# A Mamba, FP4 and attention layer in one kernel: three elementwise steps go to GpSimd, bias rows in one pass, fewer waits, and a new order on every queue

## The reference

```
xn = layernorm(x)
s  = mamba_block(xn)          # u = ln(xn)*g1+b1; xi, z = split(u @ in_proj); xc = silu(conv4(xi) + b)
                              # dt = softplus(...); h[t] = exp(dt*A)*h[t-1] + (dt*xc)[t]*B[t], 16 states
                              # y = sum_n h*C + D*xc; xn + (y*silu(z)) @ out_proj, then LN and a gelu FFN
g  = fp4_ffn(xn)              # inputs and hidden values quantized in blocks of 16; silu(gate)*up; down
x  = x + s * silu(g)
xn = layernorm(x)
s  = attention(xn)            # 16 heads; it attends over the batch axis, which has 2 entries
g  = three_residual_blocks(xn)# LoRA-folded linear + bias, LN, gelu, linear, bias, + residual
x  = x + s * silu(g)
```

## Time and profile before

| | |
|---|---|
| median of 3 runs | 1848.96 us (1847.87 to 1852.0) |
| profiled execution, its own time | 1856.52 us |
| its span, first to last instruction | 1854.7 us |
| PE busy | 1577.4 us, 85% |
| DVE busy | 1551.4 us, 84% |
| ACT busy | 1437.5 us, 78% |
| POOL busy | 1252.4 us, 68% |
| mean granted TensorE clock | 0.953 |
| rows of B and C: landing after issue | 3.3 us, 256 issues |

### The profile page before, as it was taken

How to read it: one execution, slowest core, us unless ns; L and a number is a source line. 1 busy time by engine, 2 the same in 40 slices (tenths; PEclk the granted TensorE clock), 3 DMA queues, 4 the chain that set the end, 5 groups by cost and what they waited for, 6 DMA issues and landing times.

```text
span 1854.7 us, 28175 instructions
## 1 busy us (share of the span) xinstructions
PE 1577.4 (85%) x7632; PEld 1164.4 (63%) x7632; DVE 1551.4 (84%) x2882; ACT 1437.5 (78%) x3076; POOL 1252.4 (68%) x1313
## 2 busy tenths in 40 slices
PE   0083768899999999999989999999989999999875
PEld 0051556586767677776767676767667767767653
DVE  0623999999999999999999999999999999999811
ACT  0034678898989898989889888989888989888723
POOL 0304676777777786868687777778686868787522
PEclk9976789999999999999999999999999999999987
DMA  8000111111111111111111111111111211111100
GB/s 209 0 6 29 52 47 58 47 57 37 58 48 60 43 52 51 59 47 52 52 52 52 44 51 50 58 47 46 58 52 47 63 41 58 46 44 55 35 0 12
DMA packets 68395, 91.70 MB, mean 49 GB/s; under 512 B 15674, under 2 KB 34686, under 8 KB 68238
## 3 DMA queue, kind: packets, MB, share of 16 engines
q1 hardware_dynamic: 68238, 89.91, 15.8%
...
## 4 chain that ended last, share of the span: by engine, by line
PE 27%; POOL 20%; DVE 16%; issue 16%; ACT 12%; POOLq 0%; ACTq 0%; DVEq 0%; DMA 0%
PE bank L511 10%; POOL drive L965 10%; PE bank L627 6%; DVE unit L1127 4%; DVE hc L1133 3%; PE bank L516 2%; PE y_ps L537 2%; ACT unit L742 2%; PE bank L498 1%; PE bank L563 1%; ACT op_a L709 1%; DVE xc L1158 1%; ACT L709 1%; ACT L923 1%; POOL s L1068 1%
## 5 line engine op out<-in xcount | busy, mean ns | idle before, releaser
L965 POOL TENSOR_TENSOR drive<-wx,rows 128x1024 f32<-128x1024 f32 x256 | 604.1, 2360 | 163.3 <-DVE unit L1127 82.8
L1127 DVE TENSOR_TENSOR_SCAN unit<-unit,drive 128x512 f32<-128x512 f32 x512 | 616.7, 1221 | 30.7 <-POOL drive L971 23.4
L742 ACT ACTIVATE unit<-dt,aneg 128x254 f32<-128x254 f32 x1024 | 441.9, 468 | 19.8 <-ACT carry L750 0.7
L1133 DVE TENSOR_TENSOR hc<-unit,rows 128x512 f32<-128x512 f32 x512 | 340.9, 684 | 8.8 <-issue 3.0
L537 PE MATMUL y_ps<-ident,hc 128*128 128x128 f32 x2048 | 278.1, 282 | 52.5 <-DVE hc L1133 52.4
L537 PEld LDWEIGHTS y_ps<-ident,hc 128*128 128x128 f32 x2048 | 241.2, 145 | 115.3 <-DVE hc L1133 71.8
L742 ACT ACT_TABLE_LOAD x109 | 139.8, 1283 | 3.7
L750 ACT ACTIVATE carry<-unit 128x4 f32<-128x4 f32 x512 | 79.3, 169 | 66.8 <-DVE unit L1140 63.0
L627 PE MATMUL bank<-op_a,w_f 128*128 128x256 f32 x512 | 115.7, 385 | 11.2 <-ACT op_a L709 11.2
L709 ACT ACT_TABLE_LOAD x77 | 98.8, 1283 | 22.4 <-PE bank L498 21.6
L511 PE MATMUL bank<-w_f,wide 128*128 128x256 f32 x512 | 113.3, 379 | 1.5 <-ACT wide L709 1.5
...
## 6 DMA issues: line engine op xcount, KB each, us to landing
rows<-rows_scratch SPq DMA_DIRECT2D x256, 256.0 KB, 3.3
...
```

What stands on the lines that cost most here:

```text
L742: last = a_.activation(u[:, k * TOK:(k + 1) * TOK].rearrange("p (b t) -> p b t", b=B)[:, :, 1:TC], dt[p][:, g, :].rearrange("p (b t) -> p ...
L965: g_.tensor_tensor(drive[n % 2][:, :, :].rearrange("p (g b) t -> p g b t", b=B), wx[p][:, :, :].rearrange("p g (b t) -> p g b t", b=B), ro ...
L1127: v.tensor_tensor_scan(u[:, :], u[:, :], d, 0.0, ALU.mult, ALU.add).then_inc(S["scan_done"], 1)
L1133: v.tensor_tensor(hc[n % NPROD][:, 4 * half:4 * half + 4, :].rearrange("p (g b) t -> p g b t", b=B), unit_of(ch, n, half)[:, :].rearrange( ...
```

## The change

- `wx` (dt*xc) is now a step of POOL. The addition of v to the context is the POOL step `cadd`, the addition to x the POOL step `xadd`; DVE's statistics of x become a step `x1s` that waits for it. A semaphore `ctx_ready` takes the place of the eighth count of `attn_dve`.
- A bias row is a matmul over 64 rows in the type F32R: rows 0 to 5 of `b_two` hold the biases, rows 32 to 37 what rounding them to that type leaves, and `pick` selects both. The preparation has four more loads, a memset and five small DVE instructions for it.
- Waits that an earlier instruction of the same queue implies are left out: `dt_ready` but for the first exp, `wx_ready` but for drive 0, `carry_in` but for states 0 and 8, `drive_ready` and `y_summed` in the b halves, `rows_in` at `hc`.
- All five plans are new. Everything of the arithmetic and of the buffers stays.

```diff
@@ -72,37 +73,38 @@
 
 
 PE_PLAN = """
-    b0a-- xp kv-- sum8- dt0 hqT0- q-- b0T-- sum9- v1-- dt1 b0b-- sum10- hqT1- hqT2- sum11- ctxT-- h1T-- b2b---
-    b1a-- sum12- sum13- dn- sum14- b1T-- sum15- ao-- xqT ygT0- skip ygT1- g00 sum0 g01 op- g10 sum1 g11 b1b--
-    u00 u01 sum2 u10 u2T- u11 sum3 h2T-- f10- f11- f12- f13- b2a-- uT+ sum4 sum5 f2- b2T-- xi0+ xi1+ sum6 z0+
-    sum7 xn1T- xi2+ xi3+ z1+
+    xi3 z1 b0a-- kv-- xp sum8- hqT0- dt0 q-- b0T-- sum9- v1-- hqT1- dt1 sum10- b0b-- sum11- h1T-- hqT2- ctxT--
+    b1a-- sum12- b2b--- sum13- dn- sum14- b1T-- sum15- ao-- ygT0- ygT1- skip xqT op- g00 g01 sum0 u00 b1b-- u01
+    sum1 g10 g11 u10 u2T- sum2 u11 sum3 h2T-- f10- f11- sum4 f12- f13- uT+ b2a-- sum5 f2- b2T-- xi0+ xi1+ sum6
+    sum7 z0+ xn1T- xi2+
 """
 ACT_PLAN = """
-    exp12a- hq1- hq2- out11a- exp12b- out11b- h1-- exp13a- ctx-- out12a- out12b- exp13b- out13a- exp14a- exp14b-
-    usave dtln gatec--- out13b- exp15a- out14a- exp15b- first out14b- exp0a b1n-- gatem- b1g-- out15a- exp0b
-    out15b- s1-- yg0- xq exp1a out0a out0b exp1b yg1- exp2a out1a exp2b g00 out1b g01 exp3a out2a exp3b g10
-    out2b g11 exp4a out3a opn- out3b exp4b xn+ xhf+ u2- h2-- exp5a out4a exp5b f10- f11- out4b f12- exp6a out5a
-    f13- exp6b out5b u+ exp7a b2n-- out6a exp7b out6b exp8a out7a exp8b b2g-- tap0+ tap1+ hn- z0+ xn1- tap2+
-    tap3+ z1+ out7b out8a xc0+ xc1+ exp9a exp9b out8b exp10a b0n- kv- xp+ out9a out9b exp10b exp11a dt0+ out10a
-    exp11b hq0 b0g- aexp- dt1+ out10b v1- dtexp+
+    out10b- dtexp hq1- h1-- exp12a- out11a- out11b- exp12b- exp13a- hq2- out12a- out12b- exp13b- ctx-- exp14a-
+    dtln out13a- b1n-- out13b- exp14b- exp15a- out14a- exp15b- gatec--- gatem- b1g-- first s1-- out14b- yg0-
+    out15a- yg1- exp0a exp0b out15b- xq exp1a out0a exp1b g00 out0b out1a g01 usave exp2a exp2b out1b exp3a opn-
+    g10 out2a g11 out2b exp3b exp4a u2- out3a out3b exp4b h2-- out4a xn+ exp5a exp5b f10- xhf+ f11- f12- out4b
+    f13- exp6a out5a exp6b out5b exp7a u+ out6a exp7b b2n-- out6b exp8a out7a exp8b b2g-- tap0+ tap1+ out7b hn-
+    z0+ tap2+ out8a xn1- tap3+ z1+ xc0+ xc1+ exp9a out8b exp9b exp10a kv- out9a exp10b out9b b0n- xp+ hq0 out10a
+    exp11a dt0+ exp11b b0g- aexp- v1- dt1+
 """
 POOL_PLAN = """
-    drive14- drive15- b1-- arg fix0 drive0 xout fin--- drive1 drive2 hb1-- drive3 fix1 f+ drive4 op- drive5 j0in
-    hb2-- drive6 s0b- drive7 b2-- drive8 j0out j1in x1- drive9 drive10 diff- j1out b0- hb0- drive11 xin+ drive12
-    drive13 log+
+    drive13- cadd-- log b1-- drive14- drive15- wx arg fin--- xout fix0 drive0 drive1 drive2 op- hb1-- drive3
+    drive4 f+ drive5 j0in s0b- drive6 fix1 j0out drive7 b2-- j1in drive8 xadd- hb2-- x1- drive9 hb0- diff-
+    drive10 j1out b0- drive11 xin+ drive12
 """
 DVE_PLAN = """
-    clr15a- xround yg- scan0a clr15b- hc0a scan0b clr0a hc0b clr0b scan1a hc1a clr1a scan1b scan2a hc1b clr1b
-    hc2a scan2b clr2a hc2b op- clr2b scan3a scan3b h2-- hc3a hc3b clr3a clr3b ug0 scan4a scale0 ug1 hc4a scan4b
-    clr4a hc4b scan5a clr4b scan5b hc5a xscale+ hc5b clr5a clr5b round0 scan6a b2s-- hc6a scale1 scan6b clr6a
-    hc6b scan7a hc7a clr6b scan7b clr7a hc7b clr7b x1- scan8a conv0+ scan8b hc8a hc8b clr8a conv1+ round1 b0s-
-    clr8b scan9a scan9b hc9a hc9b clr9a clr9b scan10a hc10a scan10b clr10a scan11a score- scan11b hc10b hc11a
-    clr10b hc11b clr11a attn- clr11b h1- scan12a hc12a scan12b hc12b clr12a clr12b scan13a hc13a clr13a f++
-    scan13b b1s- hc13b clr13b scan14a scan14b hc14a hc14b clr14a clr14b dt+ scan15a wx+ scan15b hc15a hc15b
+    scan12b- hc12b- scan13a- b1s-- hc13a- clr12a- clr12b- scan13b- f+ clr13a- hc13b- clr13b- dt scan14a-
+    scan14b- hc14a- hc14b- clr14a- scan15a- clr14b- scan15b- hc15a- hc15b- clr15a- yg- xround clr15b- scan0a
+    scan0b hc0a clr0a hc0b op- scan1a hc1a scan1b clr0b hc1b clr1a h2-- clr1b scan2a scan2b ug0 hc2a scan3a hc2b
+    clr2a clr2b scale0 hc3a clr3a scan3b hc3b clr3b scan4a ug1 hc4a scan4b clr4a hc4b scan5a hc5a clr4b scan5b
+    hc5b clr5a xscale+ round0 scan6a hc6a b2s-- clr5b clr6a scale1 scan6b hc6b clr6b scan7a hc7a scan7b clr7a
+    x1- hc7b x1s- scan8a clr7b scan8b hc8a conv0+ hc8b clr8a conv1+ round1 clr8b b0s- scan9a scan9b hc9a clr9a
+    hc9b clr9b scan10a scan10b hc10a clr10a scan11a score- scan11b hc10b hc11a hc11b clr10b clr11a attn- h1-
+    scan12a clr11b hc12a
 """
 SP_PLAN = """
-    rows8- rows11- load+ rows10- rows12- rows13- wr rows14- rows15- rows0 rows1 rows3 rows2 store--- rows4
-    again- rows6 rows5 rows9 rows7
+    rows5-- rows7-- rows6-- rows8-- rows10-- rows9-- again--- rows12-- rows11-- load rows13-- wr- rows15--
+    rows0- rows14-- rows3- rows2- store---- rows1- rows4-
...
-    x_diff=1, attn_dve=8, attn_exp=2, final_ready=2, stored=16,
+    x_diff=1, attn_dve=7, ctx_ready=1, attn_exp=2, final_ready=2, stored=16,
...
-        b_rows = sb("b_rows", [NROW, D])
+        b_rows = sb("b_rows", [2 * LOW, D])
+        b_two = sb("b_two", [2 * LOW, D], F32R)
+        pick = sb("pick", [2 * LOW, LOW], F32R)
...
+                *[piece for r in (0, LOW) for piece in (
+                    (b_rows[r:r + 3, :], biases.rearrange("(i k) d -> i k d", k=2)[:, 0, :]),
+                    (b_rows[r + 3:r + 4, :].rearrange("o (h d) -> o h d", d=HD),
+                     qkv_b.rearrange("(h c d) -> c h d", c=3, d=HD)[0:1, :, :]),
+                    (b_rows[r + 4:r + 5, :].rearrange("o (h d) -> o h d", d=HD),
+                     qkv_b.rearrange("(h c d) -> c h d", c=3, d=HD)[2:3, :, :]),
+                    (b_rows[r + 5:r + 6, :], ao_b[None, :]))],
...
+                    nc.gpsimd.memset(b_two[:, :].bitcast(F32), 0.0).then_inc(c_done, 1)
...
+                    v.tensor_copy(pick[0:LOW, :], ident[0:LOW, 0:LOW]).then_inc(c_prep, 1)
+                    v.tensor_copy(pick[LOW:2 * LOW, :], ident[LOW:2 * LOW, LOW:2 * LOW]).then_inc(c_prep, 1)
+                    dve.wait_ge(c_done, 6)
+                    for r in (0, LOW):
+                        v.tensor_copy(b_two[r:r + NROW, :], b_rows[r:r + NROW, :]).then_inc(c_prep, 1)
+                    dve.wait_ge(c_prep, 6 * len(quants) + 7)
+                    v.tensor_tensor(b_two[LOW:LOW + NROW, :], b_rows[LOW:LOW + NROW, :],
+                                    b_two[LOW:LOW + NROW, :].bitcast(F32), ALU.subtract).then_inc(c_prep, 1)
...
             def bias_row(dst, row, wide_):
-                return t.matmul(dst[:, 0:wide_ * D], ident[0:NROW, row:row + 1].to_broadcast([NROW, P]),
-                                b_rows[:, None, :].to_broadcast([NROW, wide_, D]), start=False, stop=True,
+                return t.matmul(dst[:, 0:wide_ * D], pick[:, row:row + 1].to_broadcast([2 * LOW, P]),
+                                b_two[:, None, :].to_broadcast([2 * LOW, wide_, D]), start=False, stop=True,
                                 skip_group_check=True)
...
             elif name == "ctxT":
-                pe.wait_ge(*at("attn_dve", ch))
+                pe.wait_ge(*at("ctx_ready", ch))
                 turn(dst, token_blocks(ctx_), "ctxT_full")
...
             if name[:3] == "exp":
                 n, half = int(name[3:-1]), "ab".index(name[-1])
                 u = unit_of(ch, n, half)
-                act.wait_ge(*at("dt_ready", ch))
+                if (n, half) == (0, 0):
+                    act.wait_ge(*at("dt_ready", ch))
                 act.wait_ge(*at("carry_saved", ch, 2 * n + half + 1 - NUNIT))
...
             elif name[:3] == "out":
                 n, half = int(name[3:-1]), "ab".index(name[-1])
                 act.wait_ge(*at("unit_clear", ch, 2 * n + half + 1))
-                act.wait_ge(*at("carry_in", ch, 1 + n // 8))
+                if n % 8 == 0 and half == 0:
+                    act.wait_ge(*at("carry_in", ch, 1 + n // 8))
...
             elif name == "v1":
                 act.wait_ge(*full("v1", ch))
-                act.wait_ge(*at("attn_dve", ch - 1))
+                act.wait_ge(*at("ctx_ready", ch - 1))
                 a_.activation(v1[:, :], dense("v1", ch)[:, 0:D], ACT.Copy).then_inc(S["v1_copied"], 1)
...
             if name[:5] == "drive":
                 n = int(name[5:])
                 pool.wait_ge(*rows_in(ch, n))
-                pool.wait_ge(*at("wx_ready", ch))
+                if n == 0:
+                    pool.wait_ge(*at("wx_ready", ch))
                 pool.wait_ge(*at("scan_done", ch, 2 * n - 2))
...
                 pool.wait_ge(*at("drive_ready", ch, 2 * n + 1))
-                pool.wait_ge(*at("carry_in", ch, 1 + n // 8))
+                if n % 8 == 0:
+                    pool.wait_ge(*at("carry_in", ch, 1 + n // 8))
                 g_.tensor_tensor(drive[n % 2][:, :, 0], drive[n % 2][:, :, 0], fix[:, n, :], ALU.add)\
                     .then_inc(S["drive_ready"], 1)
+            elif name == "wx":
+                pool.wait_ge(*at("dt_ready", ch))
+                pool.wait_ge(*at("xc_ready", ch))
```

(41 more changed lines are left out.)

6 lines of the change are left out of this document (removed).

## The result

The changed kernel takes 2121.1 us (four runs, 2119.95 to 2133.73) against 1849.5 us before: ratio 1.148, 95% interval 1.144 to 1.153. The forecast was 2065, with its own range 2025 to 2110 and the stated one 1985 to 2130.

What follows compares the result with a forecast made beforehand. DVE's queue was taken as the kernel's clock: 96.15 - 2.6 + 19.85 = 113.4 us a repeat, 13.75 more. Fifteen repeats (206) and the last chunk (+10) gave 2072.5, stated as 2065, own range 2025 to 2110, stated range 1985 to 2130.

Steps and rivals of the forecast that it cites:

- A: At scan0a, after xround: DVE has only a clear while POOL runs xout, fix0, drive0 and its carry addition; 3.95 us.
- B: At scan2a: ACT needs 2.98 us after clr1a, DVE has h2 and a clear, 0.75; a stall of 2.25 us.
- D: At scan5a: ACT's out, xn and exp after clr4a take 2.12 us against one DVE product, 0.69; 1.45 us.
- F: At x1s, DVE's statistics of x: waits for POOL's addition and two hand-overs, behind hc7b; 0.8 us.
- G: At conv1: PE's xi2 and taps and ACT's xn1 copy after conv0, about 2.7 us against DVE's 1.06; 1.65 us.
- I: At scan12a, directly after h1: PE's transposes, ACT's copy and exp, and a bank that ACT frees late; 2.65 us.
- L: At scan14b: ACT's 7.35 us after exp13b, including a load between Ln and exp, against DVE's about 5.4; 1.95 us.
- M: At yg, straight after hc15b: DVE waits for PE's last sum, where xround stood between before; 1.05 us.
- small: Three smaller stalls of DVE, at scan3b, scan6a and attn, estimated together at 1.35 us a repeat.
- Rival 2: PE's granted clock falls to about 0.79, stalls holding matmuls grow: a repeat of 118 us or more, 2135; chance 0.12.
- Rival 1: Same direction, smaller: only the forced stalls, some shortened by leaner waits; a repeat of 109.5 us, 2007; chance 0.18.
- the others: Faster, DVE's shorter list decides: 1807 us, chance 0.06; or no change, most stalls covered by each other: 1849, chance 0.03.

Runs made afterwards that it cites:

- Experiment 1: The changed kernel's work in the five plans of the kernel before, with only the three moved steps placed: 1878.0 us, ratio 1.0135 to the kernel before.
- Experiment 5: Changed kernel with SyncE issuing the second load of x first in its period instead of behind five row loads: 2137.4 us, ratio 1.155.
- 8: The changed kernel's work in the order of the kernel before, with dt*xc kept on DVE and both additions on POOL: 1856.3 us, ratio 1.0009.
- 4: Changed kernel with one step moved on POOL, xout behind drive0 instead of ahead of fix0: 2156.7 us, ratio 1.165.
- 6: Changed kernel with ACT's two exponentials of state 12 ahead of the last down-projection copy and the copy of h1: 2126.4 us, ratio 1.149.
- 7: Changed kernel with DVE's rounding of x (xround) ahead of the gating of y (yg): 2134.4 us, ratio 1.152.
- 10: Changed kernel with conv0 on DVE ahead of clr7b, scan8b and hc8a: 2124.7 us, ratio 1.148.
- 11: Changed kernel with the second load of x first, state 12's exponentials and conv0 earlier, and 44 zero matmuls on PE: 2110.3 us, ratio 1.140.

## Why the prediction was right, and where it was off

The mechanism was right: the new orders leave DVE without work between a clear and the scan that needs ACT's or POOL's answer to it. Experiment 1 shows it from outside, the stalls from inside. The time itself came in with some luck: 2121 lies above the forecast's own range (2025 to 2110) and 9 us inside the stated one, and one of the four runs, 2133.73, lies outside it. The predicted slowdown, 216 us, is four fifths of the measured 272. Per step, in the short repeat:

```
step            A    B    D    F    G    H    I    J    K    L    M    small
predicted, us  3.95 2.25 1.45 0.8  1.65 1.1  2.65 0.5  1.15 1.95 1.05 1.35
measured, us   3.98 2.30 1.38 2.04 3.76 1.07 2.46 0.30 1.14 1.57 1.12 1.05
```

(L is 0.71 before dt and 0.86 before scan14b; small is what is left of 22.2.)

*The size.* Predicted 19.85 us of stalls and a repeat of 113.4, measured 22.2 and 115.9, and 117.1 as the mean of the 13. Two terms were mis-sized. **F** was 0.8 and is 2.04: I costed SyncE's order at 0, but `again`, the second load of x, stood behind six row loads that wait for hc, was issued at 1386.49, and POOL's addition to x waited for it until 1390.66. Experiment 5 took away just that 1.2 us. **G** was 1.65 and is 3.76: the transposes and xi2, xi3 behind conv0 ran at a granted clock of 0.50, after PE had idled 3.62 us, and xi2 and xi3 took 3.70 us instead of 1.94. The remaining 1.2 us to the mean are mostly repeats in which the clock fell at other places as well.

The rows for F, of SyncE and POOL:

```profile
1386.49 0.39 SPq L1297 DMA_DIRECT2D x<-in_L_attn_x_dram  x1
```

```profile
1390.66 1.28 POOL L1079 TENSOR_TENSOR x<-x,s 128x512 f32<-128x512 f32 x1 [2.35 <-DMA x<-in_L_attn_x_dram]
```

And for G, PE in the short repeat, its window, and the same step in the long repeat:

```profile
1397.86 1.12 PE L512 MATMUL bank<-ident,h 128*128 128x128 f32 x4 [3.62 <-DVE xc L1194]
1398.77 3.70 PE L577 MATMUL bank<-u_t,w_in 128*128 128x262 f32 x8
```

```profile
1397.00:1400.00 3.00, 2.14 (x7) 1.93 (x8) 1.85 (x6) 0.76 (x2) 1.09 (x2) 0.50 0.03 11
```

```profile
1163.48 1.94 PE L577 MATMUL bank<-u_t,w_in 128*128 128x262 f32 x8
```

The changed kernel holds its own test of this. In its three long repeats, where xi2 and xi3 ran at full clock and took 1.94 us, DVE waits 1.71 us before the conv, which is the 1.65 of the prediction; in the other ten it is 3.2 to 3.8. So the chain of G was priced rightly, and its error is the clock.

*Off DVE.* I gave the three moved pieces their full 2.6 us. Experiments 1 and 8 show that in the order before they return nothing, and in the changed kernel it is about half: there the addition that makes dt takes 2259 ns beside a drive, 1225 before, and DVE's busy time fell by 20 us, not 42. This error is in the term "- 2.6" of the repeat; in the repeat of the table dt happened to take 1.22 (there it was POOL's drive that took 3.43 instead of 2.36), which is why the sum still fits. In 12 of the 16 chunks dt takes 2.4 us or more.

*Bias rows.* I took a quarter of the time; it is half: 96 rows take 47.4 us, where 192 records took 100.9. For the end of the run that made no difference, because in the changed kernel PE has 21 us idle a repeat. In the order before, it is worth 13 us.

```profile
L530 PE MATMUL bank<-b_two,pick 64*128 64x512 f32 (+1 forms) x96 | 47.4, 494 | 0.0
```

*Table loads.* 16 a repeat, as counted. Between Ln and the next exponential there is a load, as L charged it. ACT in the changed kernel:

```profile
1439.03 1.06 ACT L832 ACTIVATE wide<-wx 128x1024 f32<-128x1024 f32 x1
1439.99 0.16 ACT L766 ACTIVATE carry<-unit 128x4 f32<-128x4 f32 x1
1440.05 1.02 ACT L736 ACTIVATE xht<-bank,b_sm 128x256 f32<-128x256 f32 x2
1440.94 0.18 ACT L766 ACTIVATE carry<-unit 128x4 f32<-128x4 f32 x1
1441.14 1.28 ACT L757 ACT_TABLE_LOAD   x1
```

The exponential behind it starts at 1442.44, 0.02 us after the load. The Trainium skill (ScalarE: Activation LUTs, Table sets: the hidden batching unit) has one set for both functions; by it this load would not be there, and the trace doesn't agree. The drain of about 1.38 us that the Trainium skill puts on top of a load (ScalarE: Activation LUTs, What ACT_TABLE_LOAD costs) doesn't show here either.

*The rivals.* Rival 2, the clock, happened in part: 0.93 to 0.97 in the repeats, not 0.79, and not spread out but in stretches of 3 to 7 us at 0.50. For the same reason PE's busy time in a repeat isn't the 90.5 us of the prediction but 94.9, 82% of it. Rival 1 was too low, the others far off.

*What I would have got wrong next.* The sum of stalls gave the time, but no single stall gave time back: 4, 5, 6, 7 and 10 were each expected to gain 20 to 60 us, and gained nothing. In 4 the repair delayed another queue, in 7 it ran into contention, in 10 it moved a clear that something else needed, in 5 and 6 the clock fell more often. Only in 11, with the clock held in most repeats, do stalls shrink together, 4.1 us of them, and 1.9 us of that reached the repeat, with ten zero matmuls fewer beside it. Why an earlier x makes the clock fall ahead of prod in all repeats instead of a few is open; no run here tests it.
